# Rewriting the last node pass of a four-layer graph network: pairs of steps for the small factors, deeper run-ahead, one PSUM pair per step

## The chip, the core and the metric

The kernel runs on one core of one Trainium2 chip. The metric is the device time in microseconds (us) of one execution. TensorE (PE), VectorE (DVE), ScalarE (ACT) and GpSimd (POOL) are the computing engines, SyncE (SP) issues most DMAs. All data is f32.

## The reference, cut to what matters

50,000 nodes with 256 features, 25,000 edges sorted by target, four graph layers, each followed by a residual addition and a layer norm. The change touches the pass over the nodes that ends layer 3 (and, by being split from it, the text of the pass that ends layer 2). For layer 3:

```
h = x @ W.T                         (4 heads of 64)
e = leaky_relu(a_s[src] + a_d[dst]) over the edges and one loop per node
out = sum over e of softmax(e) * h[src]
x_new = layernorm( x + ( elu(out + bias) + x ) )
```

The edges' part of the softmax is in a table before this pass starts: per node a row of 256 unnormalised sums, 4 sums of weights (columns SC) and 4 maxima (columns MC). The pass joins the loop of the node itself to it: with e_self = leaky_relu(l + r), m = max(M, e_self), w0 = exp(M - m), w1 = exp(e_self - m), the two shares are c0 = w0 / (s*w0 + w1 + 1e-16) for the table's row and c1 = w1 / (the same) for the node's own h. Then out = c0*table + c1*h, and y = layernorm(elu(out) + 2x).

## The kernel before, in words

Phases follow each other with a barrier on all engines: the edges and nodes of layers 0 and 1, then an edge pass, a node pass, an edge pass and a node pass for layers 2 and 3. `node_pass(L, ...)` (from line 1333) writes both node passes, with branches on `L`; the last pass is `L == 3`. It takes NS = 98 steps of 512 nodes, 4 nodes a partition (J = 4), so that a tile is 128x1024. Each engine has its own program, which `run_beats` unrolls to loops of four steps (a step is a "beat", `k.s` its number), and all order comes from the semaphores written by hand: `r["elu"]`, `r["r"]`, `r["mv"]`, `r["y"]` and so on count finished pieces.

In the last pass, of step k:

- SP (`n_sync`): loads x rows (L1395, into `xt`), the h rows (L1401, into `ht`) and the table (L1404, into `tt`), four buffers each, and stores `y` (L1385) five steps behind.
- DVE (`n_vector`): `factors3` (L1564 to L1572, five operations on 128x16), then after ACT's exp `shares3` (L1578 to L1586, four operations) that give `cc`. Both are made for step k+2 inside step k, `factors3` between the `bn_stats` (L1613) and the `bn_aggr` (L1619), `shares3` behind these. Ahead of them stand the elu (L1604, PSUM and SBUF in, PSUM out), the residual sum (L1607) and `shift` of step k-1 (L1593, on 128x4).
- ACT (`n_scalar`): in this order the exp of the factors of k+2 (L1486), `normed` of k-1 (L1474, four operations), and relu and exp of k+1 (L1463, L1465), all in its one queue.
- POOL (`n_gpsimd3`): `rstd` of k (L1510, L1513), then the two products of k+2 (L1537, each 128x1024, both inputs in SBUF).
- PE (`n_tensor3`): adds the two products in PSUM by multiplying them with the identity (L1437); the sum goes to bank pair 0 or 1 of four, the elu's result to pair 2 or 3. PE waits until the elu of k-2 has been made, since that frees the pair.

Of the kernel before, what the change touches and what calls it, by code (L numbers as in the profile page):

```python
# [79 lines left out]
def gnn_program(nc, x, src, dst, ea256, ea64,  # L80
# [7 lines left out]
    P = 128  # L88
# [54 lines left out]
    with ctx:  # L143
# [1189 lines left out]
        def node_pass(L, xin, xout, H):  # L1333
            fresh()
            HD = D // H
# [11 lines left out]
            if L == 2:  # L1347
                xT = take([FH, STEP])
                hs = take([NB, J, HW])
            else:  # L1350
                ht = take([NB, J, HW])
                l1 = take([J, H])
                es = take([J, H])
                mm_ = take([J, H])
                dd = take([2, J, H])
                ww = take([2, J, H])
                t1 = take([J, H])
                den = take([J, H])
                cc = take([2, 2, J, H])
                oS = take([2, J, D])  # L1360
                oh = take([2, J, D])
            r = dict(nodes, **(nodes2 if L == 2 else nodes3))
            Z = (L - 2) * NS
            Z4 = [(L - 1) * n for n in USES]
            GD = [(CS + NG - 1 - b) // NG + (b == 0) for b in range(NG)]

            def slot_wait(eng, sems, k, extra):

                b = k.slot(NB)
                wait(eng, sems[b], 16 * (k.turn(NB) + Z4[b] + extra))  # L1370

            def out_wait(eng, k):

                b = k.slot(NB)
                if L == 2:
                    wait(eng, n_w[b], 32 * k.turn(NB) + 16 * USES[b])
                else:
                    wait(eng, n_w[b], 16 * k.turn(NB) + 48 * USES[b])

            def n_sync(sp):  # L1380
                def store(k):
                    b = k.slot(NB)
                    sp.wait_ge(r["y"], J * (k.s + Z + 1))
                    a, n = node_view(xout, k)
                    sp.dma_start(a, y[0:n, b, :, :]).then_inc(n_w[b], 16)  # L1385
                    if L == 2:
                        sp.wait_ge(r["hs"], k.s + 1)
                        a, n = node_view(h3_d, k)
                        sp.dma_start(a, hs[0:n, b, :, :]).then_inc(n_w[b], 16)

                def body(k):
                    b = k.slot(NB)
                    wait(sp, r["r"], k.s + Z - NB + 1)
                    a, n = node_view(xin, k)
                    sp.dma_start(xt[0:n, b, :, :], a).then_inc(n_x[b], 16)  # L1395
                    if L == 2:
                        wait(sp, r["elu"], k.s - NB + 1)
                    else:
                        wait(sp, r["oh"], k.s - NB + 1)
                        a, n = node_view(h3_d, k)  # L1400
                        sp.dma_start(ht[0:n, b, :, :], a).then_inc(gd[b], 16)  # L1401
                        wait(sp, r["oS"], k.s - NB + 1)
# [7 lines left out]
                for b in range(NB):  # L1410
                    sp.wait_ge(n_w[b], 48 * USES[b] if L == 2 else 64 * USES[b])

            def n_tensor2(pe):
# [15 lines left out]
            def n_tensor3(pe):  # L1429
                def body(k):  # L1430
                    b = 2 * k.slot(2)
                    pe.wait_ge(r["oS"], k.s + 1)
                    pe.wait_ge(r["oh"], k.s + 1)
                    wait(pe, r["elu"], k.s + Z - 1)
                    for i in range(2):
                        for n, a in enumerate((oh, oS)):
                            last = pe.matmul(psum[:, b + i, :], ident[:, :], a[:, k.slot(2), 2 * i:2 * i + 2, :].rearrange("p j d -> p (j d)"),  # L1437
                                             start=(n == 0), stop=(n == 1))
                    last.then_inc(r["o"], 1)
                run_beats(pe, NS, body, NB)  # L1440

            def sums(k):

                if L == 2:
                    return tt[:, k.slot(NB), :, 0:D]
                b = 2 * k.slot(2)
                return psum[:, b:b + 2, :].rearrange("p a (j d) -> p (a j) d", d=D)

            def unit(k):

                if L == 2:
                    return rr[:, k.slot(2), :, :]
                b = 4 + 2 * k.slot(2)
                return psum[:, b:b + 2, :].rearrange("p a (j d) -> p (a j) d", d=D)

            def relu_exp(act, k):
                b = k.slot(2)
                if L == 2:
                    slot_wait(act, n_t, k, 1)
                else:  # L1460
                    act.wait_ge(r["o"], k.s + 1)
                wait(act, r["elu"], k.s + Z - 1)
                act.activation(ex[:, b, :, :], sums(k), ACT.Relu, scale=-1.0).then_inc(r["mn"], 1)  # L1463
                act.wait_ge(r["mn"], k.s + Z + 1)
                act.activation(ex[:, b, :, :], ex[:, b, :, :], ACT.Exp, scale=-1.0).then_inc(r["ex"], 1)  # L1465

            def normed(act, k):
                b = k.slot(2)
                act.wait_ge(r["nm"], k.s + Z + 1)
                out_wait(act, k)  # L1470
                if L == 2:
                    wait(act, r["tr"], k.s - NB + 1)
                for j in range(J):
                    act.activation(y[:, k.slot(NB), j, :], rr[:, b, j, :], ACT.Identity, bias=nm[:, b, j:j + 1], scale=rsd[:, b, j:j + 1]).then_inc(r["y"], 1)  # L1474

            def n_scalar(act):
# [5 lines left out]

                def exps(k):
                    act.wait_ge(r["d"], 2 * (k.s + 1))
                    wait(act, r["cc"], k.s)
                    act.activation(ww, dd, ACT.Exp).then_inc(r["w"], 1)  # L1486

                if L == 3:
                    exps(beat(0, NB))
                    exps(beat(1, NB))  # L1490
                relu_exp(act, beat(0, NB))

                def body(k):
                    if L == 3 and live(k.plus(2), NS):
                        exps(k.plus(2))
                    if not (k.known() and k.s == 0):
                        normed(act, k.plus(-1))
                    if live(k.plus(1), NS):
                        relu_exp(act, k.plus(1))
                    if L == 2 and not (k.known() and k.s == 0):  # L1500
                        evac(k.plus(-1))
                run_beats(act, NS, body, NB)
                normed(act, beat(NS - 1, NB))
                if L == 2:
                    evac(beat(NS - 1, NB))

            def rstd(pool, k):
                b = k.slot(2)
                pool.wait_ge(r["mv"], J * (k.s + Z + 1))
                pool.tensor_tensor(out=ve, in0=mv[:, b, :, 1], in1=lneps[:, :], op=ALU.add).then_inc(r["ve"], 1)  # L1510
                wait(pool, r["y"], J * (k.s + Z - 1))
                pool.wait_ge(r["ve"], k.s + Z + 1)
                pool.tensor_tensor(out=rsd[:, b, :], in0=ve, in1=expo[:, :], op=ALU.pow).then_inc(r["rs"], 1)  # L1513

            def n_gpsimd2(pool):
# [6 lines left out]
                for s in range(NS):  # L1522
                    rstd(pool, beat(s, NB))
# [6 lines left out]

            def n_gpsimd3(pool):
                def shared(k):
                    b = k.slot(2)
                    pool.wait_ge(r["cc"], k.s + 1)
                    wait(pool, r["o"], k.s - 1)
                    for i, a, t, done in ((1, oh, ht, "oh"), (0, oS, tt, "oS")):
                        pool.tensor_tensor(out=a[:, b, :, :].rearrange("p j (h c) -> p j h c", h=H), in0=t[:, k.slot(NB), :, 0:D].rearrange("p j (h c) -> p j h c", h=H),  # L1537
                                           in1=cc[:, b, i, :, :].rearrange("p j (h a) -> p j h a", a=1).to_broadcast([P, J, H, HD]), op=ALU.mult).then_inc(r[done], 1)
                shared(beat(0, NB))
                shared(beat(1, NB))  # L1540

                def body(k):
                    rstd(pool, k)
                    if live(k.plus(2), NS):
                        shared(k.plus(2))
                run_beats(pool, NS, body, NB)

            def n_vector(v):
# [8 lines left out]
                def factors3(k):  # L1557

                    c0 = 6 * k.s
                    slot_wait(v, n_t, k, 1)  # L1560
                    b = k.slot(NB)
                    wait(v, gd[b], 16 * (k.turn(NB) + GD[b] + 1))
# [130 lines left out]
```

## Time and profile before

| | us |
|---|---|
| median of 3 runs | 6238.54 (6237.86 to 6242.16) |
| the profiled execution: its own time | 6242.73 |
| its span, first to last instruction | 6240.2 |
| first DMA issue of the last node pass | 5298.77 |
| first and last elu (L1604) of that pass | 5320.3 and 6228.7 |

Over the whole span PE is busy 70%, DVE 60%, POOL 59%, ACT 32%, and the mean granted TensorE clock is 0.853 of full speed. These are means over phases with different limits; the rows below are of the last pass, which takes 15% of the span. A timeline row gives the start, the duration in us, engine, line, operation, output and inputs, and in brackets how long the engine had been idle and what released it.

### The profile page before, as it was taken

To read this page: it belongs to the slowest core of one execution; us is meant where nothing else is said; L and a number is where in the kernel's file an instruction comes from. 1 tells how busy PE (TensorE), PEld (TensorE's weight loads), DVE (VectorE), ACT (ScalarE), POOL (GpSimd) and SP (SyncE) were. 2 spreads that over 40 slices of the span, in tenths; PEclk is the share of its full clock that TensorE was granted. 3 is DMA by queue.
4 is the path that set the end of the run, shared out by engine and by line. 5 is a ranking of instruction groups with operands and counts; after the bars stand their busy time and mean duration, and the time that the engine had idled before them with its cause. 6 is when DMAs were issued, how large, how long until landed. Compare 5 with 4: busy or idle time off the path is not lost. (4 is left out here: it accounts for less than half of the span.)

```text
span 6240.2 us, 71314 instructions
## 1 busy us (share of the span) xinstructions
PE 4395.5 (70%) x16758; PEld 2857.5 (46%) x16758; DVE 3753.9 (60%) x10131; ACT 1988.6 (32%) x3345; POOL 3687.1 (59%) x3371
## 2 busy tenths in 40 slices
PE   1566649989999999999997777577772000566665
PEld 0344425556666666666665666555552000222222
DVE  1344435656666666666664677577775554565665
ACT  0111125532222222222222222277772000444444
POOL 2378854445555555555555677477777776555554
PEclk5777769999999999999999888799996555777777
DMA  9977779953333333333332444399994332666665
GB/s 359 378 150 140 130 184 365 365 199 111 122 116 118 120 112 123 114 119 120 114 124 72 128 127 131 112 304 304 306 303 135 92 92 88 235 227 228 228 227 190
DMA packets 497942, 1125.26 MB, mean 180 GB/s; under 512 B 165814, under 2 KB 248714, under 8 KB 497814
## 3 DMA queue, kind: packets, MB, share of 16 engines
q1 hardware_dynamic: 346380, 913.22, 42.2%
q0 software_dynamic: 113184, 174.84, 11.8%
q10 hardware_dynamic: 38250, 35.85, 1.9%
q8 instruction: 36, 0.59, 0.0%
q14 instruction: 92, 0.75, 0.0%
HBM read 623.20 MB, written 543.83 MB: 187 GB/s over the span
## 5 line engine op out<-in xcount | busy, mean ns | idle before, releaser
L1437 PE MATMUL psum<-arena,ident 128*128 128x512 f32 x784 | 554.9, 875 | 379.7 <-DVE psum L1604 238.8
L942 PE MATMUL psum<-arena,W1b 128*128 128x512 f32 x1568 | 725.3, 605 | 0.0
L965 PE MATMUL psum<-W2b,arena 128*128 128x256 f32 x3136 | 725.2, 379 | 0.0
L730 DVE TENSOR_SCALAR arena<-arena 128x256 f32<-128x256 f32 x784 | 462.3, 650 | 302.1 <-POOL arena L725 302.1
L536 PE MATMUL psum<-arena 128*128 128x324 f32 x980 | 370.3, 547 | 367.1 <-DVE arena L456 248.2
L965 PEld LDWEIGHTS psum<-W2b,arena 128*128 128x128 f32 x3136 | 573.1, 190 | 66.3 <-issue 0.5
L855 ACT ACTIVATE arena<-psum,hbias 128x512 f32<-128x512 f32 x392 | 269.3, 687 | 860.2 <-PE psum L942 860.2
L1437 PEld LDWEIGHTS psum<-arena,ident 128*128 128x128 f32 x784 | 209.6, 279 | 724.3 <-issue 479.4
L1425 PE MATMUL psum<-Wg,arena 128*128 128x264 f32 x1568 | 399.5, 411 | 174.0 <-ACT arena L1481 174.0
L1081 POOL DMA_INDIRECT tab<-arena,IDX x392 | 398.8, 1017 | 175.3 <-issue 88.4
L1520 POOL DMA_INDIRECT ad_d<-arena,FE x392 | 425.5, 1086 | 113.2 <-issue 113.2
L942 PEld LDWEIGHTS psum<-arena,W1b 128*128 128x128 f32 x1568 | 281.7, 189 | 429.9 <-issue 429.9
L819 POOL DMA_INDIRECT xd_d<-arena,FE x392 | 411.9, 1051 | 106.2 <-issue 105.9
L1474 ACT ACTIVATE arena<-arena 128x256 f32<-128x256 f32 x784 | 405.6, 588 | 190.0 <-DVE arena L1593 190.0
L721 POOL TENSOR_TENSOR arena<-arena,lneps 128x4 f32<-128x4 f32 x196 | 39.1, 199 | 714.4 <-DVE arena L717 711.7
L536 PEld LDWEIGHTS psum<-arena 128*128 128x128 f32 x980 | 233.8, 244 | 487.9 <-issue 379.3
L1425 PEld LDWEIGHTS psum<-Wg,arena 128*128 128x128 f32 x1568 | 306.2, 200 | 249.9 <-ACT arena L1481 197.4
L408 POOL DMA_INDIRECT tab<-arena x196 | 324.7, 1657 | 147.1 <-issue 54.8
L1141 PE MATMUL psum<-ident,arena 128*128 128x128 f32 x24 | 5.8, 433 | 547.8 <-DVE arena L1293 535.9
L1537 POOL TENSOR_TENSOR arena<-arena 128x1024 f32<-128x1024 f32 x196 | 368.2, 1899 | 15.9 <-DVE arena L1586 15.9
L918 PE MATMUL psum<-W2a,arena 128*128 128x256 f32 x1568 | 356.2, 380 | 23.0 <-ACT arena L841 23.0
L683 PE MATMUL psum<-arena,W1a 128*128 128x512 f32 x784 | 354.0, 595 | 0.0
(207 smaller groups left out, 9046.2 us busy)
## 6 DMA issues: line engine op xcount, KB each, us to landing
arena<-tab SPq DMA_DIRECT2D x194, 544.0 KB
arena<-in_x SPq DMA_DIRECT2D x194, 512.0 KB, 4.6
x_d<-arena SPq DMA_DIRECT2D x194, 512.0 KB, 7.5
arena<-x_d SPq DMA_DIRECT2D x194, 512.0 KB, 5.3
tab<-zero SPq DMA_DIRECT2D x132, 486.0 KB
tab<-blank SPq DMA_DIRECT2D x97, 544.0 KB
h_d<-arena SPq DMA_DIRECT2D x97, 528.0 KB, 4.6
arena<-h_d SPq DMA_DIRECT2D x97, 528.0 KB, 4.3
```

The source lines that it names most:

```text
L536: last = pe.matmul(psum[:, 2 + j, 0:TW0], same[:, k.slot(2), i, j * P:(j + 1) * P], msg[:, k.slot(NX), i, :], start=(i == j), stop=(i == J ...
L730: v.tensor_scalar(y[:, j, :], r[:, j, :], self.mv[:, j, 0:1], self.rs[:, j:j + 1], ALU.subtract, ALU.mult).then_inc(self.s["y"], 1)
L819: pool.indirect_dma_start(out=xd_d[:, :], out_offset=bass.IndirectOffsetOnAxis(ap=FE[:, s * J + j:s * J + j + 1], axis=0), in_=x2[:, s % 2 ...
L918: last = pe.matmul(outA(j), p3y[:, f, j * P:(j + 1) * P], W2a[:, f, :], start=(f == 0), stop=(f == FH - 1))
L942: last = pe.matmul(psum[:, BR + c % RING, :], W1b[:, f, c * P:(c + 1) * P], x1T[:, f, :], start=False, stop=(f == FH - 1))
L965: last = pe.matmul(outB(j), hid[:, c, j * P:(j + 1) * P], W2b[:, c, :], start=(c == 0), stop=(c == KH - 1))
L1081: pool.indirect_dma_start(out=tab[:, :], out_offset=bass.IndirectOffsetOnAxis(ap=IDX[:, 2, c:c + 1], axis=0), in_=fin[:, s % NG, j, :], in ...
L1425: last = pe.matmul(psum[:, 2 + j, 0:HW], xT[:, f, j * P:(j + 1) * P], Wg[3][:, f, :], start=(f == 0), stop=(f == FH - 1))
L1437: last = pe.matmul(psum[:, b + i, :], ident[:, :], a[:, k.slot(2), 2 * i:2 * i + 2, :].rearrange("p j d -> p (j d)"), start=(n == 0), stop ...
L1474: act.activation(y[:, k.slot(NB), j, :], rr[:, b, j, :], ACT.Identity, bias=nm[:, b, j:j + 1], scale=rsd[:, b, j:j + 1]).then_inc(r["y"], 1)
L1520: pool.indirect_dma_start(out=ad_d[:, :], out_offset=bass.IndirectOffsetOnAxis(ap=FE[:, c:c + 1], axis=0), in_=hs[:, k.slot(NB), j, D + H3 ...
L1537: pool.tensor_tensor(out=a[:, b, :, :].rearrange("p j (h c) -> p j h c", h=H), in0=t[:, k.slot(NB), :, 0:D].rearrange("p j (h c) -> p j h ...
```

## The change

`node_pass` keeps the layer 2 case alone (its branches on `L` go; its residual sum becomes a `tensor_tensor` add where it was a `scalar_tensor_tensor` with factor 1.0). A new `last_pass` holds the last pass:

- DVE: `factors` and `shares` work on the steps k and k+1 together: 32 columns where there were 16 (64 for `cc`). `factors` for steps k+4 and k+5 stands at the end of an even step k, `shares` for the same pair at the end of the following odd step. Between `bn_stats` and `bn_aggr` nothing stands any more.
- ACT: the order in a step is the exp of the pair (in odd steps), relu and exp of k+1, then `normed` of k-1.
- POOL: products for k+3 behind `rstd` of k.
- PE and PSUM: step k uses bank pair k mod 4, and the elu is written over the sum in the same pair. PE waits for the residual sum of step k-4.
- SP: the tables and h rows are issued seven steps ahead (as soon as the products of k+3 are done), the x rows four ahead, and `y` is stored two steps behind.

```diff
-                    wait(pe, r["elu"], k.s + Z - 1)
+                    wait(pe, r["r"], k.s + Z - NB + 1)
...
+            def banks(k):
+                b = 2 * k.slot(NB)
+                return psum[:, b:b + 2, :].rearrange("p a (j d) -> p (a j) d", d=D)
...
+            def l_sync(sp):
...
+                def body(k):
+                    if live(k.plus(NB), NS):
+                        rows(k.plus(NB))
+                    if not (k.known() and k.s < 2):
+                        store(k.plus(-2))
+                    if live(k.plus(NB + 3), NS):
+                        tables(k.plus(NB + 3))
...
+            def l_scalar(act):
...
+                def body(k):
+                    if k.slot(2) == 1 and live(k.plus(3), NS):
+                        exps(k.plus(3))
+                    if live(k.plus(1), NS):
+                        relu_exp(k.plus(1))
+                    if not (k.known() and k.s == 0):
+                        normed(k.plus(-1))
...
+            def l_gpsimd(pool):
...
+                def body(k):
+                    rstd(k)
+                    if live(k.plus(3), NS):
+                        shared(k.plus(3))
...
+            def l_vector(v):
...
+                def body(k):
+                    b = k.slot(2)
+                    v.wait_ge(r["ex"], k.s + Z + 1)
+                    v.scalar_tensor_tensor(out=banks(k), in0=ex[:, b, :, :], scalar=-1.0, in1=banks(k), op0=ALU.add, op1=ALU.max).then_inc(r["elu"], 1)
+                    v.wait_ge(r["elu"], k.s + Z + 1)
+                    v.wait_ge(n_x[k.slot(NB)], 16 * (k.turn(NB) + 2 * USES[k.slot(NB)] + 1))
+                    wait(v, r["y"], J * (k.s + Z - 1))
+                    v.scalar_tensor_tensor(out=rr[:, b, :, :], in0=xt[:, k.slot(NB), :, :], scalar=2.0, in1=banks(k), op0=ALU.mult, op1=ALU.add).then_inc(r["r"], 1)
+                    if not (k.known() and k.s == 0):
+                        shift(k.plus(-1))
+                    v.wait_ge(r["r"], k.s + Z + 1)
+                    wait(v, r["mv"], J * (k.s + Z))
+                    for j in range(J):
+                        v.bn_stats(st[:, j, :], rr[:, b, j, :]).then_inc(r["st"], 1)
+                    v.wait_ge(r["st"], J * (k.s + Z + 1))
+                    v.memset(gap, 0.0)
+                    for j in range(J):
+                        v.bn_aggr(mv[:, b, j, :], st[:, j, :]).then_inc(r["mv"], 1)
+                    if b == 0 and live(k.plus(4), NS):
+                        factors(k.plus(4))
+                    elif b == 1 and live(k.plus(3), NS):
+                        shares(k.plus(3))
```

## Rows read from the trace of the kernel before

**Rows 1.** Windows: stretch, its us, busy us and instructions by engine, PEclk, DMA share, GB/s.
```profile
900.00:1100.00 200.00, 200.00 (x746) 108.98 (x746) 119.90 (x139) 113.95 (x186) 92.85 (x94) 1.00 1.02 364
5350.00:6100.00 750.00, 455.53 (x640) 171.67 (x639) 454.03 (x1678) 337.12 (x560) 395.23 (x320) 0.77 0.63 229
```

**Rows 2.** Waits in 5686 to 6099: us in total, times, longest.
```profile
DVE psum L1604 <- ACT arena L1465: 151.8, 45, 4.3
```

**Rows 3.** Line L1604 in both node passes: durations in ns, first and last start.
```profile
L1604 DVE SCALAR_TENSOR_TENSOR psum<-arena,psum x98: 1228/1228/1230, 5320.3 to 6228.7; 128x1024 f32<-128x1024 f32 x98
```

**Rows 4.** Timeline of one step of the last pass.
```profile
5713.52 1.23 DVE L1604 SCALAR_TENSOR_TENSOR psum<-arena,psum 128x1024 f32<-128x1024 f32 x1 [3.10 <-ACT arena L1465]
5714.78 1.22 DVE L1607 SCALAR_TENSOR_TENSOR arena<-arena,psum 128x1024 f32<-128x1024 f32 x1
...
5715.92 0.15 DVE L1593 SCALAR_TENSOR_TENSOR arena<-arena 128x4 f32<-128x4 f32 x1
5716.03 1.41 DVE L1613 BATCH_NORM_STATS2 arena<-arena 128x6 f32<-128x256 f32 x4
...
5717.36 0.16 DVE L1564 TENSOR_TENSOR arena<-arena 128x16 f32<-128x16 f32 x1
...
5718.25 0.28 DVE L1619 BATCH_NORM_AGGREGATE arena<-arena 128x2 f32<-128x6 f32 x3
5718.27 0.23 ACT L1486 ACTIVATE arena<-arena 128x32 f32<-128x32 f32 x1 [4.78 <-DVE arena L1572]
5718.40 2.06 ACT L1474 ACTIVATE arena<-arena 128x256 f32<-128x256 f32 x4
5718.53 0.18 DVE L1578 TENSOR_TENSOR arena<-arena 128x16 f32<-128x16 f32 x1
...
5718.95 1.01 POOL L1513 TENSOR_TENSOR arena<-arena,expo 128x4 f32<-128x4 f32 x1
5719.23 0.19 DVE L1586 TENSOR_TENSOR arena<-arena 128x32 f32<-128x32 f32 x1
5719.93 3.76 POOL L1537 TENSOR_TENSOR arena<-arena 128x1024 f32<-128x1024 f32 x2
5720.37 1.00 ACT L1463 ACTIVATE arena<-psum 128x1024 f32<-128x1024 f32 x1
...
5721.40 1.06 ACT L1465 ACTIVATE arena<-arena 128x1024 f32<-128x1024 f32 x1
```

**Rows 5.** Timeline, PE: eight matmuls of one step, at low and at full clock.
```profile
5686.27 6.65 PE L1437 MATMUL psum<-arena,ident 128*128 128x512 f32 x8 [3.62 <-DVE psum L1604]
5338.16 3.70 PE L1437 MATMUL psum<-arena,ident 128*128 128x512 f32 x8 [2.28 <-POOL arena L1537]
```

**Rows 6.** Timeline of the node pass of layer 2: bn_stats with bn_aggr directly behind.
```profile
4221.02 1.41 DVE L1613 BATCH_NORM_STATS2 arena<-arena 128x6 f32<-128x256 f32 x4
...
4222.56 0.28 DVE L1619 BATCH_NORM_AGGREGATE arena<-arena 128x2 f32<-128x6 f32 x3
```

**Rows 7.** Timeline of the last pass's start, DVE beside POOL's products.
```profile
5309.89 0.35 DVE L1564 TENSOR_TENSOR arena<-arena 128x16 f32<-128x16 f32 x1 [1.73 <-DMA arena<-tab]
5310.17 1.90 POOL L1537 TENSOR_TENSOR arena<-arena 128x1024 f32<-128x1024 f32 x1
5310.27 1.82 DVE L1566 SCALAR_TENSOR_TENSOR arena<-arena 128x16 f32<-128x16 f32 x1
5328.63 1.89 POOL L1537 TENSOR_TENSOR arena<-arena 128x1024 f32<-128x1024 f32 x1
5329.71 0.83 DVE L1593 SCALAR_TENSOR_TENSOR arena<-arena 128x4 f32<-128x4 f32 x1
```

**Rows 8.** Two lines of layer 1's node pass: ns min/median/max, starts, shape.
```profile
L878 DVE TENSOR_TENSOR arena<-arena x98: 691/2626/2725, 1329.6 to 3349.9; 128x512 f32<-128x512 f32 x98
L799 POOL TENSOR_TENSOR arena<-arena,b2a x98: 2340/2346/2802, 1327.0 to 3346.0; 128x1024 f32<-128x1024 f32 x98
```

**Rows 9.** Line L1537, the products: ns min/median/max, starts, shape.
```profile
L1537 POOL TENSOR_TENSOR arena<-arena x196: 1887/1898/1905, 5308.3 to 6219.1; 128x1024 f32<-128x1024 f32 x196
```

**Rows 10.** DMA issues in 4100 to 4500: KB each, median us to landing.
```profile
x_d<-arena SPq DMA_DIRECT2D x57, 512.0 KB, 8.2
```

More of the change, by code:

```diff
@@ L1346, in node_pass @@
             gap = take([1])
[L1347 to L1370, printed above, removed]
+            xT = take([FH, STEP])
+            hs = take([NB, J, HW])
+            r = dict(nodes, **nodes2)
             def out_wait(eng, k):
                 b = k.slot(NB)
[L1375 to L1378, printed above, removed]
+                wait(eng, n_w[b], 32 * k.turn(NB) + 16 * USES[b])
             def n_sync(sp):
@@ L1442, in sums @@
[L1442 to L1471, printed above, removed]
+            def n_scalar(act):
+                def relu_exp(k):
+                    b = k.slot(2)
+                    act.wait_ge(n_t[k.slot(NB)], 16 * (k.turn(NB) + USES[k.slot(NB)] + 1))
+                    wait(act, r["elu"], k.s - 1)
+                    act.activation(ex[:, b, :, :], tt[:, k.slot(NB), :, 0:D], ACT.Relu, scale=-1.0).then_inc(r["mn"], 1)
+                    act.wait_ge(r["mn"], k.s + 1)
+                    act.activation(ex[:, b, :, :], ex[:, b, :, :], ACT.Exp, scale=-1.0).then_inc(r["ex"], 1)
+                def normed(k):
+                    b = k.slot(2)
+                    act.wait_ge(r["nm"], k.s + 1)
+                    out_wait(act, k)
@@ L1481, in evac, with n_gpsimd, rstd @@
                         act.activation(xT[:, f, :], psum[:, f, :], ACT.Copy).then_inc(r["xT"], 1)
[L1483 to L1491, printed above, removed]
+                relu_exp(beat(0, NB))
                 def body(k):
[L1494 to L1495 removed]
                     if not (k.known() and k.s == 0):
[L1497 removed]
+                        normed(k.plus(-1))
                     if live(k.plus(1), NS):
[L1499 to L1500 removed]
+                        relu_exp(k.plus(1))
+                    if not (k.known() and k.s == 0):
                         evac(k.plus(-1))
                 run_beats(act, NS, body, NB)
[L1503 to L1515, printed above, removed]
+                normed(beat(NS - 1, NB))
+                evac(beat(NS - 1, NB))
+            def n_gpsimd(pool):
+                def rstd(k):
+                    b = k.slot(2)
+                    pool.wait_ge(r["mv"], J * (k.s + 1))
+                    pool.tensor_tensor(out=ve, in0=mv[:, b, :, 1], in1=lneps[:, :], op=ALU.add).then_inc(r["ve"], 1)
+                    wait(pool, r["y"], J * (k.s - 1))
+                    pool.wait_ge(r["ve"], k.s + 1)
+                    pool.tensor_tensor(out=rsd[:, b, :], in0=ve, in1=expo[:, :], op=ALU.pow).then_inc(r["rs"], 1)
                 def to_edges(k):
@@ L1555, in to_rows, with shift @@
                                     in1=bias3[:, :].rearrange("p (a d) -> p a d", a=1).to_broadcast([P, J, HW]), op=ALU.add).then_inc(r["hs"], 1)
-                def factors3(k):
-                    c0 = 6 * k.s
-                    slot_wait(v, n_t, k, 1)
-                    b = k.slot(NB)
-                    wait(v, gd[b], 16 * (k.turn(NB) + GD[b] + 1))
-                    M = tt[:, b, :, MC:MC + H]
-                    v.tensor_tensor(out=l1, in0=ht[:, b, :, D:D + H], in1=ht[:, b, :, D + H:D + 2 * H], op=ALU.add).then_inc(r["small"], 1)
+                def shift(k):
+                    b = k.slot(2)
+                    v.wait_ge(r["rs"], k.s + 1)
+                    v.scalar_tensor_tensor(out=nm[:, b, :], in0=mv[:, b, :, 0], scalar=-1.0, in1=rsd[:, b, :], op0=ALU.mult, op1=ALU.mult).then_inc(r["nm"], 1)
@@ new lines, in body @@
+                def body(k):
+                    b = k.slot(2)
+                    v.wait_ge(r["ex"], k.s + 1)
+                    wait(v, r["y"], J * (k.s - 1))
+                    v.scalar_tensor_tensor(out=rr[:, b, :, :], in0=ex[:, b, :, :], scalar=-1.0, in1=tt[:, k.slot(NB), :, 0:D], op0=ALU.add, op1=ALU.max).then_inc(r["elu"], 1)
+                    v.wait_ge(r["elu"], k.s + 1)
+                    v.wait_ge(n_x[k.slot(NB)], 16 * (k.turn(NB) + USES[k.slot(NB)] + 1))
+                    v.tensor_tensor(out=rr[:, b, :, :], in0=xt[:, k.slot(NB), :, :], in1=rr[:, b, :, :], op=ALU.add).then_inc(r["r"], 1)
+                    if not (k.known() and k.s == 0):
+                        shift(k.plus(-1))
+                    v.wait_ge(r["r"], k.s + 1)
+                    wait(v, r["mv"], J * k.s)
+                    for j in range(J):
+                        v.bn_stats(st[:, j, :], rr[:, b, j, :]).then_inc(r["st"], 1)
+                    v.wait_ge(r["st"], J * (k.s + 1))
+                    v.memset(gap, 0.0)
+                    for j in range(J):
+                        v.bn_aggr(mv[:, b, j, :], st[:, j, :]).then_inc(r["mv"], 1)
+                    if not (k.known() and k.s < 2):
+                        to_rows(k.plus(-2))
@@ L1593, in shift @@
                     v.scalar_tensor_tensor(out=nm[:, b, :], in0=mv[:, b, :, 0], scalar=-1.0, in1=rsd[:, b, :], op0=ALU.mult, op1=ALU.mult).then_inc(r["nm"], 1)
-                if L == 3:
-                    for s in range(2):
-                        factors3(beat(s, NB))
-                        shares3(beat(s, NB))
+                for s in (0, 2):
+                    factors(beat(s, NB))
+                    shares(beat(s, NB))
                 def body(k):
@@ L1613, in body @@
                         v.bn_stats(st[:, j, :], rr[:, b, j, :]).then_inc(r["st"], 1)
-                    if L == 3 and live(k.plus(2), NS):
-                        factors3(k.plus(2))
                     v.wait_ge(r["st"], J * (k.s + Z + 1))
```

235 lines of the change are left out of this document (160 added, 75 removed).

## The prediction

> **What bounds the kernel now.** I read the windows first, to see whether the stage is short of bandwidth or of an engine, then the waits of the stage, then one step of its timeline. The windows show the last pass with no engine full: of 750 us PE has 456, DVE 454, POOL 395, ACT 337, and DMA moves 229 GB/s at a share of 0.63, while another stage reaches 364 GB/s at a share of 1.0 [rows 1]. So a loop of waits sets the pace. The step: first and last elu lie 908.4 us apart over 97 intervals, 9.365 us each [rows 3]. The waits name the loop: DVE stands 151.8 us of 413 at the elu, for ACT's exp [rows 2]. The timeline shows why [rows 4]: ACT's queue holds the small exp (L1486) in front, which waits for `factors3` that DVE makes behind its bn_stats. From the elu at 5713.52 DVE works 4.7 us until that exp may start (5718.27); then ACT has normed 2.06, relu 1.00 and exp 1.06, which end at 5722.46, and the next elu can start. That is 8.9 to 9.0 us. One step in four, PE's sum is late on top of it: eight matmuls take 6.65 us at a granted clock of 1.2 GHz against 3.70 at 2.4 GHz [rows 5], and PE starts only once the elu two steps back is made.
>
> **The change, loop by loop.** Zero is the end of a step's bn_aggr (5718.53 in [rows 4]); P is the step's period.
>
> *The old loop goes.* The small exp depends on factors made a step earlier and relu/exp of k+1 stands ahead of normed of k-1, so neither waits for this step's DVE work. ACT's load in a step is 2.06 + 2.09 + half of about 0.26 (0.23 at 32 columns, now 64, estimated), 4.3 us: under all that follows.
>
> *DVE alone.* Elu to residual sum 1.26, to shift 1.14, to bn_stats 0.11 [rows 4]; bn_stats to the end of bn_aggr 1.82 with nothing between them [rows 6]. The pair work: the five factor operations took 5717.36 to 5718.27, 0.9 us; the four of the shares 5718.53 to 5719.42, also 0.9. Going from 16 to 32 columns costs 0.18 to 0.19 [rows 4], so I take 0.02 more for each and 0.03 for the 64-column one: about 0.9 to 1.0 from the first to where the next elu can start. Each step now holds one of the two. Sum 1.26 + 1.14 + 0.11 + 1.82 + 0.95 = 5.3 us.
>
> *POOL alone.* End of bn_aggr to L1513 0.42, to the first product 0.98, products 3.76 [rows 4]: 5.16 us.
>
> *DMA alone.* A step moves 512 + 512 + 528 + 544 KB = 2.146 MB. At 364 GB/s [rows 1] that is 5.9 us. The Trainium skill (SBUF — State Buffer, section Summary: rules for kernel authors) gives about 358 GB/s for HBM to SBUF; by it the floor would be 6.0 us, 10 us more over the pass, and the trace's own 364 decides.
>
> *The loop over three steps.* Products for k+3 end 5.16 after bn_aggr of k; PE adds 3.7 (6.65 at low clock), relu and exp 2.1, normed of k+1 behind them 2.1, then residual sum to bn_aggr 1.14 + 0.11 + 1.82 = 3.1; with 0.2 of hand-overs 16.4 us (19.3 at low clock) for three steps: 5.5 to 6.4 us a step.
>
> *The port, which I take to decide.* At the start of the pass DVE's small operations once met the products. A 128x16 one with both inputs in SBUF, started at 5310.27, took 1.82 us where it takes 0.18, and ended with the product, at 5312.09 against 5312.07; the shift at 5329.71 took 0.83 for 0.15 and ended at 5330.54, the product at 5330.52 [rows 7]. In layer 1's pass L878, both inputs in SBUF, has a median of 2.63 us and a minimum of 0.69, beside a 2.35 us POOL operation on SBUF [rows 8]. The products themselves never stretch: 1.887 to 1.905 in 196 [rows 9]. Elu and residual sum have one input in PSUM and keep 1.23 and 1.22 beside the products (the product that starts at 5328.63 runs beside the residual sum before that shift). So: a DVE operation with two SBUF inputs that starts during a product waits for its end. Now place the shift. POOL is idle at zero, products run 1.40 to 3.26 and 3.26 to 5.16 (1.86 from start to start, being 3.76 less 1.90). DVE: pair work to about 0.90 (0.80 to 1.00), elu, 1.26 later (1.36 in some steps) the residual sum, 1.14 later the shift: at 3.30, between 3.20 and 3.50. In the old step the shift comes 4 us before the products; now it comes as the second product begins. A shift ahead of 3.26 passes between the two products, as the L1564 that ended at 5310.24 did [rows 7]; one behind it ends at 5.18. Then bn_stats starts at 5.11 (it starts 0.04 to 0.07 before the shift ends) and bn_aggr ends 1.82 later: P = 6.93. Of the interval 3.20 to 3.50 four fifths lie behind 3.26, and any lateness of elu or residual sum (exp, x rows) pushes the shift deeper into the second product without changing its end. So I take the blocked case for every step. At P = 6.93 all else has room: 2.146 MB in 6.93 us is 310 GB/s; POOL is free from 5.16; the three-step loop needs at most 19.3 of 20.8 us.
>
> The Trainium skill (SBUF — State Buffer, section Who interferes with whom) says that of a DVE instruction with two SBUF inputs and a GpSimd instruction reading SBUF the one issued second blocks fully, and that an instruction with at most one SBUF input does not contend. Had the port been shared in halves, the shift would take some 0.3 us and the step would be 5.9; rows 7 speak for the full block.
>
> *PSUM.* The elu in place, same pair read and written, is not in the trace. Nearest row: 1.23 us with different pairs. Bounds: no gain, and 1.23 more; either way it is hidden, since the shift at 3.3 or 4.5 ends at 5.18. I take 0. Only in the unblocked case would it cost.
>
> *SP's queue.* h rows and table of k+7 wait for the products of k+3 (3.3 and 5.2 after zero), with x rows and the store behind them in the queue; x rows are four steps ahead and lose nothing. The tables are wanted by the factors at 2P = 13.9 at the earliest, so landing may take 8.2 us from 5.7. Landings here are unknown at this load; the nearest long one is 8.2, a store in layer 2's pass [rows 10]. I take 0; the bound is a rival below.
>
> *Layer 2's pass.* The residual sum as tensor_tensor: 16-column ones of either kind take 0.16 to 0.18, the rate is the same; 0, within 0.02 x 98 = 2 us.
>
> *Ends of the pass.* At the start factors need two steps' tables (about 1 us more), and `factors` of steps 2 and 3 fall into products (one operation passes per product: some 2 us, hidden behind PE's first sum, 5.97 us at low clock); the first intervals run unblocked. At the end, steps 96 and 97 have no products beside them: up to 2.6 less each. I take 0 net, within 5 us.
>
> **Sum.** 97 x (9.365 - 6.93) = 236 us. From the profiled execution, 6242.7 (span 6240.2 and 2.5 around it), that gives 6006.5. The median of the runs lies 4.2 us below that execution, so I forecast 6002.
>
> **Rivals.**
> 1. *The shift slips through.* If sequencer and semaphore gaps put it before 3.26, or it passes otherwise, the step falls to the DMA floor, 5.9 (the three-step loop can lift it to 6.4). 97 x 3.47 = 336: 5902; at 6.4 about 5951, which is also where a pass ends in which three in ten of the shifts slip (a step that does takes 5.3, and 0.7 x 6.93 + 0.3 x 5.3 is 6.4). For: 0.04 to 0.2 us decide. Against: DMA or exp lateness, frequent at P = 5.9, throws the shift back into the product.
> 2. *Tables land late.* Above 8.2 us of landing the factors wait and half of the excess goes into each step: at 11 us P = 8.3, 6135. For: one queue carries everything. Against: 229 GB/s now goes with idle DMA, and 310 is still below 364. The same price stands for ACT's order: relu of k+1 held by a late sum holds normed behind it.
> 3. *Slower.* The products give way too. They were never stretched while DVE's two-input operations were few beside them; now shift, factors and shares contend. The blocked step is 1.40 + two products + 1.77, so it reaches 9.365 when one product takes 3.10 us instead of 1.88, and at 3.6 it is 10.4: 100 us slower, 6338. Against: rows 7 and 9, in which POOL held its time.
> 4. *The loop is not broken:* if steps stay near 9.3 through a wait I have missed, 6238.
>
> **Chances.** Forecast, 6.6 to 7.2 a step (5971 to 6029): 0.55. Rival 1: 0.27. Rival 2 and the like, 7.2 to 9.1: 0.10. Rival 4: 0.03. Rival 3: 0.05. A difference under 0.2% (12 us) can't be told from none. Faster 0.92, same 0.03, slower 0.05. The range reaches from the floor, 5.75 a step (364 GB/s is a mean; 4% better), 5888, to 7.5 a step, 6058.
>
> **What would show it.** L1593's successor at about 1.9 to 2.0 us instead of 0.15 in nearly all steps and ending with the second product; POOL idle near 1.7 us a step; DMA near 310 GB/s; elu at 1.23; almost no wait of DVE for ACT's exp. Wrong, if the shift stays at 0.15 and DVE waits for a DMA (rival 1), if DVE's waits name the table's DMA or ACT (rival 2), or if products exceed 1.9 us (rival 3).

## The result, and the profile after

The changed kernel takes 5973.4 us (median of 4 runs, 5964.5 to 5984.4) against 6240.4 (6237.9 to 6245.0) for the kernel before: 267 us less, a ratio of 0.957 with a 95% interval of 0.956 to 0.959. The forecast was 6002, 236 us less. A second comparison on another chip gave 0.958 (0.957 to 0.959).

The first view is the profiled execution of the changed kernel by stretches, as in [rows 1]; the second its elu, shift and products by line, as in [rows 3, 9].

```profile
5350.00:5950.00 600.00, 387.07 (x728) 150.35 (x728) 551.00 (x1503) 380.30 (x591) 447.31 (x365) 0.91 0.92 317
```

```profile
L1701 DVE SCALAR_TENSOR_TENSOR psum<-arena,psum x98: 1205/1222/1230, 5314.9 to 5949.8; 128x1024 f32<-128x1024 f32 x98
...
L1693 DVE SCALAR_TENSOR_TENSOR arena<-arena x98: 153/1218/1902, 5322.4 to 5956.4; 128x4 f32<-128x4 f32 x98
...
L1636 POOL TENSOR_TENSOR arena<-arena x196: 1892/1903/1955, 5303.3 to 5941.9; 128x1024 f32<-128x1024 f32 x196
```

Elu to elu is (5949.8 - 5314.9) / 97 = 6.545 us where it was 9.365 [rows 3]: 97 x 2.82 = 273.5 us. The two spans differ by 278.0, 11 us more than the medians, because the profiled execution of the changed kernel is the fastest of its four. Of the 4.5 us that the steps leave over, 6.7 us is that the last pass happened to start earlier (first DMA issue at 5292.1, was 5298.8; the elu of the layer 2 pass already starts 6.0 us earlier), while its start and end cost 2.2 us more. DVE now looks 92% busy, but a part of that is no work: the shift, 128x4 elements, has a median of 1.22 us where it was 0.15 in [rows 4]. The products did not stretch. The mean granted clock of the stretch is 0.91, was 0.77.

Among the waits in 5350 to 5900 the elu's for ACT's exp, 151.8 us in [rows 2], is down to 1.3:

```profile
PE psum L1587 <- POOL arena L1636: 193.4, 76, 4.1
ACT arena L1604 <- PE psum L1587: 148.9, 64, 6.0
POOL arena L1642 <- DVE arena L1715: 123.4, 65, 4.4
...
DVE psum L1701 <- issue: 6.6, 21, 0.3
DVE arena L1705 <- ACT arena L1613: 6.4, 15, 0.8
...
DVE arena L1665 <- DMA arena<-tab: 5.4, 9, 0.9
DVE psum L1701 <- ACT arena L1606: 1.3, 1, 1.3
```

PE, ACT and POOL wait, for something that goes back to DVE; DVE waits for almost nothing, and a list of waits does not show a wait inside an instruction. The timeline does. This is a step with the shift blocked (bn_aggr had ended at 5505.05):

```profile
5505.96 1.22 DVE L1701 SCALAR_TENSOR_TENSOR psum<-arena,psum 128x1024 f32<-128x1024 f32 x1
...
5506.45 3.76 POOL L1636 TENSOR_TENSOR arena<-arena 128x1024 f32<-128x1024 f32 x2
5507.21 1.22 DVE L1705 SCALAR_TENSOR_TENSOR arena<-arena,psum 128x1024 f32<-128x1024 f32 x1
...
5508.35 1.88 DVE L1693 SCALAR_TENSOR_TENSOR arena<-arena 128x4 f32<-128x4 f32 x1
...
5510.15 1.39 DVE L1711 BATCH_NORM_STATS2 arena<-arena 128x6 f32<-128x256 f32 x4
...
5511.68 0.28 DVE L1715 BATCH_NORM_AGGREGATE arena<-arena 128x2 f32<-128x6 f32 x3
```

Products from 1.40 to 5.16 after bn_aggr, the shift there at 3.30 and gone at 5.18, the next bn_aggr at 6.91: the forecast's step, which had 6.93. Two steps on (bn_aggr ended at 5518.87) the shift comes 3.19 after it, passes between the products, and its step takes 5.13:

```profile
5520.27 3.77 POOL L1636 TENSOR_TENSOR arena<-arena 128x1024 f32<-128x1024 f32 x2
...
5522.06 0.15 DVE L1693 SCALAR_TENSOR_TENSOR arena<-arena 128x4 f32<-128x4 f32 x1
...
5523.72 0.28 DVE L1715 BATCH_NORM_AGGREGATE arena<-arena 128x2 f32<-128x6 f32 x3
```

In the whole pass 69 of 98 shifts were blocked, 90.9 us in all, and each of the 69 ended 0.02 us after a product. Of the other 29, 21 slipped between the two products, five came after both, in steps whose elu was late, and three, at the end of the pass, had no products beside them. Mostly it is a pattern of four: blocked by 1.7, 1.5, let through, blocked by 1.1. The steps are then three of 6.91 and one of 5.13, mean 6.47 (from elu to elu they repeat as 6.45, 6.98, 6.73 and 5.70, with the same mean). What decides is small: the factors' first operation starts 0.08 us before the end of bn_aggr in the step that slips and 0.01 before it in the step with the shift at 3.30; why these two differ is not shown. The remaining 0.08, from 6.47 to 6.545, comes from a few long steps. In this one, 10.7 us from elu to elu, the table is late by 0.7 us, POOL starts its products while the factors are half done, and two of them wait 1.9 us each:

```profile
5449.72 0.19 DVE L1665 TENSOR_TENSOR arena<-arena 128x32 f32<-128x32 f32 x1 [0.72 <-DMA arena<-tab]
5449.95 0.19 DVE L1667 SCALAR_TENSOR_TENSOR arena<-arena 128x32 f32<-128x32 f32 x1
5450.18 0.19 DVE L1669 TENSOR_TENSOR arena<-arena 128x32 f32<-128x32 f32 x1
5450.39 3.76 POOL L1636 TENSOR_TENSOR arena<-arena 128x1024 f32<-128x1024 f32 x2
5450.40 1.94 DVE L1672 TENSOR_TENSOR arena<-arena 128x32 f32<-128x32 f32 x1
5452.27 1.94 DVE L1673 TENSOR_TENSOR arena<-arena 128x32 f32<-128x32 f32 x1
...
5454.13 1.22 DVE L1701 SCALAR_TENSOR_TENSOR psum<-arena,psum 128x1024 f32<-128x1024 f32 x1
```

### The profile page after: what moved, and what is told of

The parts are those of the page before. It is cut to its first block and busy times, and to the rows that moved or that the text cites. A ratio compares the mean times of both kernels' runs of the same rounds, so it can differ in the third digit from the quotient of the medians.

```text
span 5962.2 us, 70229 instructions
## 1 busy us (share of the span) xinstructions
PE 4250.6 (71%) x16758; PEld 2804.5 (47%) x16758; DVE 3789.0 (64%) x9690; ACT 1985.4 (33%) x3296; POOL 3685.6 (62%) x3371
## 5 line engine op out<-in xcount | busy, mean ns | idle before, releaser
L1587 PE MATMUL psum<-arena,ident 128*128 128x512 f32 x784 | 416.0, 682 | 246.4 <-POOL arena L1636 246.4
L1587 PEld LDWEIGHTS psum<-arena,ident 128*128 128x128 f32 x784 | 161.8, 217 | 499.8 <-issue 471.8
L633 POOL DMA_INDIRECT fe_d<-EID,FIRST x196 | 200.0, 1020 | 242.7 <-ACT arena L658 197.7
```

## The experiments

Steps are mean intervals from first to last elu of the pass, worked out as above. Ratios are to the kernel before on the same chip.

| kernel | step, us | median, us | ratio (95%) |
|---|---|---|---|
| changed kernel, first chip | 6.545 | 5973.4 | 0.9573 (0.9559 to 0.9587) |
| elu twice (e_elu_twice) | 6.955 | 6005.9 | 0.9636 (0.9620 to 0.9652) |
| ACT's order as before (e_act_order) | 6.953 | 6004.1 | 0.9629 (0.9613 to 0.9646) |
| shift behind bn_aggr (e_shift_late) | 6.436 | 5954.8 | 0.9557 (0.9541 to 0.9573) |
| shift on GpSimd (e_shift_pool) | 6.600 | 5965.2 | 0.9566 (0.9550 to 0.9582) |
| half of the x rows (e_half_rows) | 6.536 | 6060.2 | 0.9569 (0.9552 to 0.9586) |
| shift behind bn_aggr, half of the x rows (e_late_half) | 6.092 | 6013.5 | 0.9508 (0.9482 to 0.9533) |
| unit in PSUM pairs of its own (e_unit_apart) | 6.586 | 6060.1 | 0.9569 (0.9552 to 0.9587) |
| before, with the new ACT order (e_before_order) | 10.225 | 6414.1 | 1.0132 (1.0114 to 1.0149) |
| changed kernel again | 6.607 | 6059.0 | 0.9581 (0.9568 to 0.9594) |
| shift behind bn_aggr again | 6.495 | 6047.1 | 0.9556 (0.9543 to 0.9570) |
| the same, table wait ahead of bn_aggr (e_late_wait) | 6.334 | 6043.4 | 0.9554 (0.9541 to 0.9567) |
| before, new ACT order, y wait behind the elu (e_before_order_y) | 9.615 | 6352.7 | 1.0046 (1.0031 to 1.0062) |

The kernel before took 6235.6 us beside the second to the fifth line. From the sixth line on the runs are from chips on which it took 6327 and 6326 us; the profile of the changed kernel there has the longer time ahead of the pass (first elu at 5404.9, where it is 5314.9 on the first chip), so steps and ratios are compared, not times.

**Is the shift's block what sets the step?** More work was put ahead of the shift:

```diff
+                    v.scalar_tensor_tensor(out=banks(k), in0=ex[:, b, :, :], scalar=-1.0, in1=banks(k), op0=ALU.add, op1=ALU.max).then_inc(r["twice"], 1)
+                    v.wait_ge(r["twice"], k.s + 1)
                     v.scalar_tensor_tensor(out=banks(k), in0=ex[:, b, :, :], scalar=-1.0, in1=banks(k), op0=ALU.add, op1=ALU.max).then_inc(r["elu"], 1)
```

> After the change, with the elu made twice in each step of the last pass (the second gives the same result), 1.23 us more work for VectorE ahead of the shift. Theory A (the port): the shift reaches its place 1.25 us later, still inside the second product, and ends with it as before; only the one step in four in which it slips through is lost, so every step takes about 6.9 us instead of 6.55 on average: 97 x 0.36 = 35 us more, about 6008. Rival B (the step is VectorE's own work): 97 x 1.23 = 119 us more, about 6092. Rival C (the step is the DMA's): no change, 5973.

Measured: 6.955 us a step, 6005.9. 120 us of VectorE work were added and the pass grew by 97 x 0.41 = 40 us. Nearly all of it is the lost slips: no shift passes between the products any more, and where it now comes later it still ends with the second product. Only in one step of four does it come after the second product has all but ended (5.13 after bn_aggr), and that step takes 7.16. A step of this kernel's timeline:

```profile
5503.07 3.76 POOL L1636 TENSOR_TENSOR arena<-arena 128x1024 f32<-128x1024 f32 x2
5503.72 1.23 DVE L1703 SCALAR_TENSOR_TENSOR psum<-arena,psum 128x1024 f32<-128x1024 f32 x1
5504.98 1.22 DVE L1707 SCALAR_TENSOR_TENSOR arena<-arena,psum 128x1024 f32<-128x1024 f32 x1
5506.12 0.73 DVE L1693 SCALAR_TENSOR_TENSOR arena<-arena 128x4 f32<-128x4 f32 x1
5506.77 1.39 DVE L1713 BATCH_NORM_STATS2 arena<-arena 128x6 f32<-128x256 f32 x4
```

It ends at 5506.85, the product at 5506.83. Theories B and C fall.

**The shift elsewhere.** First behind bn_aggr (with one more wait on GpSimd, for its own `rs`, so that `ve` is not written early), then on GpSimd:

```diff
-                    if not (k.known() and k.s == 0):
-                        shift(k.plus(-1))
                     v.wait_ge(r["r"], k.s + Z + 1)
...
                         v.bn_aggr(mv[:, b, j, :], st[:, j, :]).then_inc(r["mv"], 1)
+                    if not (k.known() and k.s == 0):
+                        shift(k.plus(-1))
```

> After the change, with the shift of step k-1 moved from ahead of bn_stats to behind bn_aggr of step k; same instructions. Theory A: bn_stats and bn_aggr run while the second product runs, the shift then waits 0.1 to 0.5 us at most, and the step falls to the next bound, DMA at 5.9 or the three-step loop at 5.5 to 6.1: about 5.95 us a step, 97 x 0.6 = 58 us less, about 5915 (5895 to 5935). Rival B (VectorE's own work): the same work, no change. Rival C (DMA, at a share of 0.92 to 0.96 now): at most 10 us less.

```diff
                     pool.tensor_tensor(out=rsd[:, b, :], in0=ve, in1=expo[:, :], op=ALU.pow).then_inc(r["rs"], 1)
+                    pool.tensor_tensor(out=mneg, in0=zero[:, 0:J], in1=mv[:, b, :, 0], op=ALU.subtract).then_inc(r["mneg"], 1)
+                    pool.wait_ge(r["mneg"], k.s + 1)
+                    pool.wait_ge(r["rs"], k.s + Z + 1)
+                    pool.tensor_tensor(out=nm[:, b, :], in0=mneg, in1=rsd[:, b, :], op=ALU.mult).then_inc(r["nm"], 1)
...
-                    if not (k.known() and k.s == 0):
-                        shift(k.plus(-1))
...
+                    wait(v, r["nm"], k.s + Z - 1)
```

> After the change, with the shift computed on GpSimd (two operations on 128x4 behind the rstd) instead of on VectorE. Theory A: VectorE has no operation with two SBUF inputs beside the products except factors and shares; GpSimd's chain grows from 5.16 to about 5.8, so the step is 5.9 to 6.1 us: 97 x 0.55 = 53 us less, about 5920. Rival B: 0.11 us a step less, about 5962. Rival C: no change.

Both missed: 6.436 and 6.600 us a step instead of 5.95 and 6.0 (on GpSimd even no better than the changed kernel). With the shift behind bn_aggr no shift was blocked at all (0.13 us in every step but the first and last) and half the steps took 5.3 to 5.9; but 19 took 7.3 to 10.3. The stall was not removed, it moved into the factors. The kernel with the shift on GpSimd has the same long steps, 12 above 8.3 us, and DVE waits for the table 19 times, 24.1 us. In the timeline of the kernel with the shift behind bn_aggr:

```profile
5522.43 0.13 DVE L1694 SCALAR_TENSOR_TENSOR arena<-arena 128x4 f32<-128x4 f32 x1
...
5523.59 0.19 DVE L1666 TENSOR_TENSOR arena<-arena 128x32 f32<-128x32 f32 x1 [1.03 <-DMA arena<-tab]
5523.82 0.19 DVE L1668 SCALAR_TENSOR_TENSOR arena<-arena 128x32 f32<-128x32 f32 x1
5523.99 3.77 POOL L1636 TENSOR_TENSOR arena<-arena 128x1024 f32<-128x1024 f32 x2
5524.05 1.90 DVE L1670 TENSOR_TENSOR arena<-arena 128x32 f32<-128x32 f32 x1
5525.98 1.83 DVE L1673 TENSOR_TENSOR arena<-arena 128x32 f32<-128x32 f32 x1
5527.73 0.18 DVE L1674 TENSOR_TENSOR arena<-arena 128x32 f32<-128x32 f32 x1
```

A table 1.03 us late costs 1.03 and twice 1.7. DVE's waits for the table are now 16.9 us in 19 places in 5350 to 5900 (5.4 in 9 in the changed kernel), at 332 GB/s and a DMA share of 0.95 (326 and 0.95 in the changed kernel). By the time alone rival C, the DMA, would be the one that came true: it gave this edit at most 10 us, and the ratios differ by 0.0016, which is 10 us (their intervals overlap). So whether the DMA sets the step had to be tried by itself.

**Is the full DMA queue behind it?** Half of the x rows was loaded (the residual sum reads old data for the other half), in both kernels:

```diff
-                    sp.dma_start(xt[0:n, b, :, :], a).then_inc(n_x[b], 16)
+                    sp.dma_start(xt[0:n, b, 0:2, :], a[:, 0:2, :]).then_inc(n_x[b], 16)
```

> After the change as it is, with half of the x rows loaded (as in e_late_half). Theory A (the port): the pattern of four steps, 6.45, 6.98, 6.73, 5.70, mean 6.47, stays, only the few long steps of late tables go: 97 x 0.08 = 8 us less, about 5965. Rival C (the step is the DMA's): 12% less of it, 97 x 0.78 = 76 us less, about 5897.

> As e_shift_late (shift behind bn_aggr), and only half of the x rows is loaded in the last pass (256 KB a step less, 1.884 instead of 2.146 MB; the sum reads old data for the rest). In e_shift_late most steps took 5.3 to 6.0 us, but one in five 7.5 to 10.4, where the factors' first operation had waited for the table's DMA. Theory A2 (a late table pushes the factors into the products, each later one then waits for the end of a product, and tables are late because the DMA engines are full): with 12% less to move the tables are on time and nearly all steps take 5.3 to 5.7 us: 97 x (6.44 - 5.5) = 91 us less than e_shift_late's 5955, about 5864. Rival (the table's latency, not the bandwidth, makes it late): about 5950, the long steps stay.

The changed kernel nearly keeps its step with 12% less to move (6.536; 6.586 and 6.607 for its like on those chips), 74 of its 98 shifts are blocked, and only the longest steps go (7.8 us at most, where it was 10.7), as theory A had it: the DMA does not set the step, the port does. With the shift behind bn_aggr the step falls from 6.44 to 6.09, and only 4 waits for a table are left in 500 us, 2.9 us in all: late tables are a matter of bandwidth. It did not reach 5.5. In the same 500 us (5450 to 5950) DVE waited 21.2 us for normed and 17.4 us for exp, and ACT 91.9 us for PE's sums. That fits the loop over three steps, forecast at 5.5 to 6.4; it was not tested by a run of its own.

**The wait for the tables ahead of bn_aggr**, so that a late table holds POOL as well:

```diff
+                    if b == 0 and live(k.plus(4), NS):
+                        for n in (k.plus(4), k.plus(5)):
+                            t = n.slot(NB)
+                            v.wait_ge(gd[t], 16 * (n.turn(NB) + GD[t] + 1))
+                            v.wait_ge(n_t[t], 16 * (n.turn(NB) + 2 * USES[t] + 1))
                     v.wait_ge(r["st"], J * (k.s + Z + 1))
                     v.memset(gap, 0.0)
```

> As e_shift_late, and in even steps VectorE waits for the pair's h rows and tables ahead of bn_aggr instead of behind it; same instructions and transfers. Theory A2: in e_shift_late a table that is 1 us late lets GpSimd start its products first, and the factors' operations then each wait for the end of a product, 4 us in all. With the wait ahead of bn_aggr the products start later by the same 1 us and the factors run before them: the steps of 7.5 to 10.2 us (about one in five) become 6.5 to 7.5, 34 us less over the pass: a ratio to the kernel before of about 0.950 (e_shift_late 0.956). Rival (the long steps only make up for a full DMA queue): no change, 0.956.

> The kernel of e_shift_late again, beside the changed kernel on the same chip, since its gain over it (12 us between medians) lay inside the intervals of both. Theory A with A2: 6.44 us a step against 6.55, about 11 us less than the changed kernel. If the two are equal within 5 us, the shift's place is worth nothing as long as late tables take their toll.

> The changed kernel again, to compare with the two above on one chip: ratio to the kernel before 0.957, as measured.

The mechanism showed: no step above 8.3 us (twelve of 8.7 to 10.9 in the kernel without it), factors at 0.19 us each on average. The worth was not shown. In the profiles it is half of the forecast, 97 x 0.16 = 16 us, but the profiled execution is the fastest of its five, 12 us below their median, and the medians differ by 3.6 us, not told apart from none: at 335 GB/s and a share of 0.97 what was saved at the port is waited for at the tables (41 us in 500). Against the changed kernel both variants win: 6043.4 (6031.4 to 6053.1) and 6047.1 (6040.2 to 6050.0) against 6059.0 (6058.2 to 6070.6). The first, with a ratio of 0.9554 against 0.9581, is 0.3% better than the change; between the two variants these runs don't decide.

**What did the single parts do?** ACT's order put back in the changed kernel:

```diff
-                    if live(k.plus(1), NS):
-                        relu_exp(k.plus(1))
                     if not (k.known() and k.s == 0):
                         normed(k.plus(-1))
+                    if live(k.plus(1), NS):
+                        relu_exp(k.plus(1))
```

> After the change, but with ScalarE's order as before (normed of k-1 ahead of relu and exp of k+1). Theory A: the elu comes 1.6 us later in a step, the shift still falls into the second product and ends with it, so a step takes 6.9 to 7.0 us: 97 x 0.4 = 39 us more, about 6012. Rival D (the order on ScalarE gave most of the gain, so its loop decides again): shift to normed to exp to elu to shift, 0.2 + 2.06 + 2.1 + 2.4 + the blocked 1.2 to 1.9, 8 to 8.7 us a step: 6115 to 6180.

6.953 us, the number of theory A, but not by the block alone. The elu is later (DVE waits 112 us for the exp in 550), so the shift comes when the second product is almost done: 50 of 98 were blocked, by 0.27 us each, and in the other steps it comes 5.06 to 5.08 after bn_aggr and is free.

```profile
5505.28 0.43 DVE L1693 SCALAR_TENSOR_TENSOR arena<-arena 128x4 f32<-128x4 f32 x1
...
5505.82 2.08 ACT L1613 ACTIVATE arena<-arena 128x256 f32<-128x256 f32 x4 [2.83 <-DVE arena L1693]
...
5509.92 1.23 DVE L1701 SCALAR_TENSOR_TENSOR psum<-arena,psum 128x1024 f32<-128x1024 f32 x1 [1.43 <-ACT arena L1606]
```

ACT's loop is closed again: elu to shift 2.49, the shift, and from its end over normed, relu and exp to the next elu 4.20. With the shift at its 0.15 that is 6.84 us, against 6.91 for the blocked step, so this run can't tell the two apart. It does show what the new order is for: by this sum, with the old order no step could be much shorter than 6.8, even with no shift blocked. Rival D had this loop, and priced it too high by adding the whole block.

The unit in pairs of its own:

```diff
-                b = 2 * k.slot(NB)
+                b = 2 * k.slot(2)
...
-                    v.scalar_tensor_tensor(out=banks(k), in0=ex[:, b, :, :], scalar=-1.0, in1=banks(k), op0=ALU.add, op1=ALU.max).then_inc(r["elu"], 1)
+                    v.scalar_tensor_tensor(out=unit(k), in0=ex[:, b, :, :], scalar=-1.0, in1=banks(k), op0=ALU.add, op1=ALU.max).then_inc(r["elu"], 1)
...
-                    wait(pe, r["r"], k.s + Z - NB + 1)
+                    wait(pe, r["elu"], k.s + Z - 1)
```

> After the change, but with two PSUM pairs for the sums and two for the unit, as before (the elu reads one pair and writes another; PE waits for the elu of two steps back). Theory A: the products of k+3 end long after the elu of k+1, so PE waits for nothing new, the elu takes the same 1.22 us, and the time stays: 5973 within 10. Rival E (the one pair of four is what frees PE): PE waits for the elu again and sums come late, 0.5 us a step or more: 6020.

No difference (6.586 against 6.607 us), and the elu is 1.223 us in both: four pairs and writing in place are worth nothing that these runs can tell.

And the other way round, ACT's order alone in the kernel before, then the place of the wait for `y` too:

```diff
-                    if not (k.known() and k.s == 0):
-                        normed(act, k.plus(-1))
-                    if live(k.plus(1), NS):
+                    if L == 3 and live(k.plus(1), NS):
                         relu_exp(act, k.plus(1))
+                    if not (k.known() and k.s == 0):
+                        normed(act, k.plus(-1))
+                    if L == 2 and live(k.plus(1), NS):
+                        relu_exp(act, k.plus(1))
```

> The kernel before, with ScalarE's order alone changed in the last pass (relu and exp of k+1 ahead of normed of k-1). The old loop of 9.0 us loses normed's 2.06 and would give 7.15, or 7.8 with the shift blocked; but products are only two ahead, so a loop over two steps holds: bn_aggr to products 1.40, products 3.76, PE 3.7 to 6.65, relu and exp 2.1, elu to bn_aggr 5.0: 16.1 to 19 us for two steps, 8.05 to 9.5. Theory A: about 8.3 us a step, 97 x 1.05 = 102 us less than before, about 6134. Rival D (the order is the gain, the run-ahead only decoration): 7.2 to 7.8 a step, 6025 to 6085.

```diff
-                    wait(v, r["y"], J * (k.s + Z - 1))
+                    if L == 2:
+                        wait(v, r["y"], J * (k.s + Z - 1))
                     v.scalar_tensor_tensor(out=unit(k), ...
...
                     slot_wait(v, n_x, k, 1)
+                    if L == 3:
+                        wait(v, r["y"], J * (k.s + Z - 1))
```

> The kernel before, with ScalarE's order of the changed kernel, and the wait for y moved from ahead of the elu to ahead of the residual sum, as in the changed kernel. In e_before_order the elu of k+1 waited for normed of k-1, which now stood behind relu and exp, so the loop was as long as before. Theory A: with this wait behind the elu, that loop is gone and what holds is the loop over two steps, because products are two ahead: bn_aggr to products 1.40, products 3.76, PE 3.7 to 6.65, relu and exp 2.1, elu to bn_aggr 5.1: 16.2 to 19.1 for two steps, 8.1 to 9.5 us, about 8.5: 84 us less than before, ratio 0.987. Rival (run-ahead of products adds nothing): 7.2 to 7.8 a step, 150 to 210 us less, ratio 0.966 to 0.976.

Both are slower than the kernel before, by 1.3% and 0.5%, and I had both wrong by their sign. The first takes 10.2 us a step. A step of its timeline:

```profile
5810.14 2.06 ACT L1474 ACTIVATE arena<-arena 128x256 f32<-128x256 f32 x4
...
5812.23 1.23 DVE L1606 SCALAR_TENSOR_TENSOR psum<-arena,psum 128x1024 f32<-128x1024 f32 x1 [5.33 <-ACT arena L1474]
```

In the kernel before, the elu waits for `y` of two steps back, which was no wait as long as normed stood ahead of relu; now it is behind exps and relu in the queue, so the loop has all its old parts and the late sum on top. With that wait behind the elu the step is 9.6 us, just above the upper end, 9.5, of what was expected for the loop over two steps; the 8.5 in it took PE too fast and had no wait for normed ahead of the residual sum. In its timeline that wait is 0.84 us, PE's sum takes 6.17 us, and relu waits 3.75 us for it:

```profile
5800.69 1.22 DVE L1612 SCALAR_TENSOR_TENSOR arena<-arena,psum 128x1024 f32<-128x1024 f32 x1 [0.84 <-ACT arena L1474]
...
5801.87 6.17 PE L1437 MATMUL psum<-arena,ident 128*128 128x512 f32 x8 [6.99 <-POOL arena L1539]
...
5808.15 1.02 ACT L1463 ACTIVATE arena<-psum 128x1024 f32<-128x1024 f32 x1 [3.75 <-PE psum L1437]
```

So the gain is not a sum of parts: without the deeper run-ahead of the products and the factors by pairs the new order loses. These two without the order are the run above, 6.95 us. They were not tried apart from each other, so how the gain divides between them is open.

## Why the prediction was right, point by point

- *The old loop.* Right: DVE's 151.8 us of waiting for exp fell to 1.3 us. But I described it by ACT's order and the small exp alone. Two more loops lie close behind it: the wait for `y` ahead of the elu, which closes one as soon as ACT's order is changed, and the loop over two steps through the products and PE, which held the last run at 9.6 us. The order alone did not free the kernel before.
- *DVE, POOL, products.* The pieces held within about 0.1 us: blocked step 6.91 for 6.93, products 1.40 to 5.16. From bn_aggr to an elu that waits for nothing it was 0.79 to 0.97 us, where 0.80 to 1.00 and, as the usual case, 0.90 were put; the 0.79 is what lets a shift slip. The reciprocal is the one operation of the pair work that I under-priced: 0.35 us for 0.25, where 0.02 more were forecast.
- *The port.* Shown three ways: shift and product end together; 120 us of added work ahead of it cost 40; the shift moved away is 0.13 us in every step but the first and last. "Blocked in every step" was the term that was mis-sized: 7 of 10 were. The second product starts 3.26 us after bn_aggr as forecast, and the arrivals are 3.19, 3.30, 3.53 and 3.96, on both sides of it; but they repeat with the loop of four steps, so one in four slips nearly each time, at no chance of its own. That is 97 x 0.46 = 45 us less than forecast; late tables give back 97 x 0.08 = 8. Together the 37 us between 236 and 273.5. The time still fell into the band put on the forecast, 5971 to 6029, but by 2 us and with some luck: the traced step of 6.545 lies below the 6.6 that bounded it.
- *Rival 1* had the right event. Its milder case, three shifts in ten slip and 6.4 a step, comes nearest to the steps as measured (29 of 98 unblocked, 21 of them slips, 6.47 in the repeated pattern), and it stood there as a part of a rival with a chance of 0.27, not as the forecast. A step that slips takes 5.1, where 5.3 was said. Its full case had the wrong price: a pass without blocked shifts does not fall to the DMA floor of 5.9. The factors take the shift's place at the port when a table is late; with that mended it is 6.33 in the one execution profiled, the fastest of five.
- *Rival 2* happens on a small scale: landing medians rose from 3.4 us to 7.4 (x rows) and 7.9 (y), and nine pairs waited for a table. Its price was wrong: not half of the lateness for a step, but the lateness and up to two products.
- *Rival 3.* The products kept 1.90 us with 7 in 10 shifts and some factors waiting beside them.
- *PSUM, SP's queue, layer 2's pass.* Elu 1.22 in place; the tensor_tensor form takes 1.224, as the old form did in layer 2's pass. At zero, as put.

## What to carry to other kernels

An engine that looks 92% busy can be waiting inside its instructions: look for a small operation whose duration is ten times its minimum and ends with another engine's. Operations with two SBUF inputs on VectorE, even on 128x4, have to be placed with regard to when GpSimd's long SBUF operations run. A wait for a DMA ahead of the point that starts these, not behind it, kept a late load from costing two products on top; here that bought no time that the runs could tell, and the tables were waited for instead. Before changing an order of queues, list the waits of every reader again: a wait that costs nothing in the old order can close the new loop.

## What I had not expected of the hardware

A shift that came 0.04 us after the second product's start took 1.88 us and one that came 0.07 us ahead of it took 0.15: 0.11 us of arrival made steps of 6.9 and of 5.1 us. The reciprocal grew from 0.25 us at 16 columns to 0.35 at 32, while the other operations grew by 0.02 to 0.03. And PE's mean granted clock rose from 0.77 to 0.91 of full speed when the step shortened from 9.4 to 6.5 us, with the same eight matmuls in a step.
